# Graph network, three layers on one core: self edges squeezed out of the edge lists of layers 1 and 2, and no more row-by-row loads beside the indirect gathers

## The reference, cut to what matters

```python
h = x @ enc_W + enc_b                                    # 12500 x 64
for l in range(3):
    cat = concatenate([h[src], h[dst], edge_features])   # 64 + 64 + 16 columns
    m = relu(cat @ msg_W1[l] + msg_b1[l]) @ msg_W2[l] + msg_b2[l]
    agg = segment_sum(m, dst)
    h = gru_cell(agg, h, ...)                            # sigmoid, sigmoid, tanh
x = layernorm(x + relu(h @ ro_W1 + ro_b1) @ ro_W2 + ro_b2)
```

## Time and profile before

| | us |
|---|---|
| time, median of 3 (lowest, highest) | 6154.56 (6151.95, 6156.73) |
| profiled execution, first to last instruction | 9775.6 |
| PE busy | 2880.1 |
| DVE busy | 3532.6 |
| ACT busy | 346.4 |
| POOL busy | 4639.2 |

### The profile page before, as it was taken

The page is one execution under the profiler, slowest core; times in us unless marked ns, Lnnn a source line. Parts: engine busy times, 40 slices in busy tenths (PEclk is TensorE's granted clock), DMA queues, the critical chain, the costliest instruction groups (busy, mean ns, idle before and its releaser), DMA issues.

```text
span 9775.6 us, 72182 instructions
## 1 busy us (share of the span) xinstructions
PE 2880.1 (29%) x7290; PEld 1610.2 (16%) x7290; DVE 3532.6 (36%) x4656; ACT 346.4 (4%) x542; POOL 4639.2 (47%) x4865
## 2 busy tenths in 40 slices
PE   3323322322322332222222222223232222322223
PEld 2111111111111221111111111112111111111112
DVE  2333333333333433333333333333333334333334
ACT  0000000000000000000000000000000000000001
POOL 5444444444444454444444444445454445545543
PEclk6555555555555555555555555555555555555555
DMA  3111111111111111111111111111111111111111
GB/s 87 31 31 30 30 30 30 28 31 30 31 30 30 30 28 30 30 30 30 30 30 29 30 30 27 30 31 30 30 31 31 30 30 34 31 31 31 31 30 25
DMA packets 351443, 308.63 MB, mean 32 GB/s; under 512 B 149364, under 2 KB 237518, under 8 KB 350568
## 3 DMA queue, kind: packets, MB, share of 16 engines
q0 software_dynamic: 155328, 159.79, 8.6%
q1 hardware_dynamic: 118271, 110.17, 4.0%
q10 hardware_dynamic: 77328, 33.96, 1.4%
HBM read 280.52 MB, written 22.83 MB: 31 GB/s over the span
## 4 chain that ended last, share of the span: by engine, by line
SPq 57%; issue 38%; DVE 2%; PE 1%; another core or an unknown queue 1%; DMA 0%; ACT 0%; POOL 0%; DVEq 0%; ACTq 0%; POOLq 0%
SPq L473 46%; SPq L469 6%; SPq L642 2%; SPq L633 1%; SPq L527 1%; DVE work_ps L1493 1%; SPq L630 1%; DVE folds L1528 0%; DVE p_src L1490 0%; PE bank L838 0%; DMA p_src<-p_tab 0%; PE work_ps L949 0%; PE bank L962 0%; SPq L662 0%
## 5 line engine op out<-in xcount | busy, mean ns | idle before, releaser
L798 POOL DMA_INDIRECT p_src<-p_tab,idx_all x4767 | 4551.1, 955 | 4916.8 <-DVE work_ps L1493 3467.4
L962 PE MATMUL bank<-hot,folds 128*128 128x96 f32 x2496 | 660.1, 413 | 4012.9 <-issue 2053.0
L1490 DVE TENSOR_TENSOR p_src<-work_ps,p_src 128x512 f32<-128x512 f32 x624 | 427.6, 685 | 3374.9 <-DMA p_src<-p_tab 2912.1
L962 PEld LDWEIGHTS bank<-hot,folds 128*128 128x128 f32 x2496 | 532.1, 296 | 4278.5 <-issue 2198.0
L949 PE MATMUL work_ps<-w_edges,msg 128*128 128x512 f32 x1248 | 1120.0, 997 | 21.4 <-DMA windows_sb<-q_tab 21.4
L1523 DVE SCALAR_TENSOR_TENSOR work_ps<-work_ps,rel 128x1024 f32<-128x1024 f32 x624 | 768.8, 1232 | 21.5
L1493 DVE TENSOR_TENSOR work_ps<-p_src,bank 128x1024 f32<-128x1024 f32 x624 | 767.0, 1229 | 21.4
L1528 DVE TENSOR_REDUCE folds<-work_ps 128x256 f32<-128x1024 f32 x624 | 758.4, 1215 | 0.0
L959 PE MATMUL bank<-hot,counts 128*34 128x96 bf16 x416 | 68.9, 261 | 2248.6 <-issue 1278.6
L1538 DVE TENSOR_TENSOR sums<-bank,sums 128x96 f32 x624 | 158.1, 253 | 872.6 <-remote 699.5
L959 PEld LDWEIGHTS bank<-hot,counts 128*34 128x34 bf16 x416 | 27.1, 108 | 2368.2 <-issue 1359.8
(11 more groups left out here) (167 smaller groups left out, 1800.9 us busy)
## 6 DMA issues: line engine op xcount, KB each, us to landing
p_src<-p_tab ACTq DMA_DIRECT2D x9792, 0.2 KB
p_src<-p_tab SPq DMA_DIRECT2D x9792, 0.2 KB
p_src<-p_tab,idx_all POOLq DMA_INDIRECT x4830
msg<-in_edge_k SPq DMA_DIRECT2D x156, 256.0 KB
pick<-rel_tab SPq DMA_DIRECT2D x312, 96.0 KB
windows_sb<-q_tab ACTq DMA_DIRECT2D x312, 24.0 KB
windows_sb<-q_tab SPq DMA_DIRECT2D x312, 24.0 KB
pick<-q_tab ACTq DMA_DIRECT2D x312, 24.0 KB
```

The costliest lines, as they stand in the source:

```text
L798: pool.indirect_dma_start(out=p_src[r][0:rows, t, :], out_offset=None, in_=p_tab[l][0:NODES, :], in_offset=bass.IndirectOffsetOnAxis(ap=id ...
L962: last = nc.tensor.matmul(fold_ps, folds[:, b, :], hot_all[n % 2][:, s * BLOCKS + b, 1:WINDOW + 1], start=(b == 0), stop=(b == BLOCKS - 1))
L1490: nc.vector.tensor_tensor(rows, edge_ps[k % 2], rows, ALU.add).then_inc(with_edge, 1)
```

## The change

**Packs.** In layers 1 and 2 the edges are cut into 197 packs of 1080 consecutive edges. The self edge of each node is squeezed out of a pack, and what is left (at most 1024 edges) is one step. So layers 1 and 2 have 197 steps, layer 0 still 208 (`STEPS_OF`).

**Squeezing.** It is done on the DVE in layer 0, beside its steps. The edge list is laid out with a pack a partition: 100 packs in a first batch, 97 in a second. For each batch 18 planes of 1080 elements (relative destination, source, 16 features) are moved left by 7 predicated copies each, by 1, 2, 4 ... 64 elements; masks `moves` say which elements take part. `press_step(m)` gives every step of layer 0 its share: 16 steps of a batch make the masks (`prepare`), and then 4 steps a plane: two copies, two, three, and one that turns the plane (`press_plane`). That is 22 groups a batch, 44 of 52 groups in all. SP stores the planes to HBM (`pack_store`), loads the next (`pack_load`), and brings indices and destinations back into SBUF in 8 pieces (`piece_load`), from which `make_masks` makes the masks.

**Self edges.** Their message needs no gather, as source and destination are one node: `h` times (source part + destination part) of the weights, plus the features. Their features are picked out in layer 0 (`select_loops`, a group at a time; two more matmuls and one more DVE add a step) and kept in free rows of `state`. In layers 1 and 2 a chunk has one stage more, -1: a matmul with `loop_w` and a relu on ACT; the DVE adds it to the sums (`loop_added`).

**Single rows.** `single_rows` is gone from SP and ACT; every tile is gathered by GpSimd. Layer 0 has 1661 gathers, layers 1 and 2 have 1576 each.

**Start.** Before the flags are set which choose the branch, the DVE measures whether the packs are within bounds (two loads of 106 rows of the edge list, some 50 more instructions), and the PE's matmuls for the ranges come after the encoder's last unit instead of at its 20th.

```diff
+PACK = 1080
+PACKS = -(-EDGES // PACK)
+BATCHES = ((0, 100), (100, PACKS - 100))
+STEPS_OF = (STEPS, PACKS, PACKS)
...
-        def gathers_of(m):
-            return LAST_TILES if m == STEPS - 1 else EDGE_TILES - has_singles(m)
+        def gathers_of(l, m):
+            return LAST_TILES if l == 0 and m == STEPS - 1 else EDGE_TILES
...
-                    for g in range(2, GROUPS):
-                        single_rows(sp, mybir.EngineType.SP, l, GROUP * (g - 2) + GROUP - 1, 0, SP_ROWS, sp_singles)
-                        group_inputs(n0 + g, g)
+                    for g in range(2, GROUPS_OF[l]):
+                        if l == 0:
+                            batch, at = job(g - 3)
+                            if batch is not None and at >= PREP_GROUPS:
+                                pack_store(batch, at)
+                            batch, at = job(g - 1)
+                            if batch is not None and (at > PREP_GROUPS or (batch, at) == (1, 0)):
+                                pack_load(batch, at)
+                        for q in range(PIECES_ALL):
+                            if piece_loaded_at(q) == (l, g):
+                                piece_load(q)
...
+                        group_inputs(l, n0 + g, g)
                         group_windows(l, n0 + g, g)
...
-                        for at, q in pieces_at(m):
-                            single_rows(act, mybir.EngineType.Activation, l, at, SP_ROWS + q * PIECE, PIECE, act_singles)
...
-                if u == RANGES_AFTER:
-                    pe.wait_ge(vw_sb, LAYERS)
...
+            pe.wait_ge(vw_sb, LAYERS)
+            pe.wait_ge(reduced, 1)
...
+            measured_by(nc.vector.tensor_tensor(rise, pair_dst[:, RUN:], whole, ALU.subtract))
+            measured_by(nc.vector.tensor_reduce(pair_flags[0:PAIRED + 1, 0:1], rise, AX.X, ALU.max))
...
+            def select_loops(n):
...
+                nc.vector.tensor_tensor(edge_major[n % 2], edge_major[n % 2],
+                                        loop_runs[:].unsqueeze(2).to_broadcast([128, GROUP * BLOCKS, EDGE_DIM, RUN]), ALU.mult).then_inc(loop_steps, 1)
+                nc.vector.tensor_reduce(loop_sel[n % 2], edge_major[n % 2], AX.X, ALU.add).then_inc(looped, 1)
...
+            def shift(what, k, count):
+                low, high, by = PASS_LOW[k], PASS_HIGH[k], 1 << k
+                squeeze(nc.vector.copy_predicated(what[0:count, low:high], moves[k][0:count], what[0:count, low + by:high + by]))
...
+            def press_plane(batch, at, part):
...
+                if part < 2:
+                    shift(what, 2 * part, count)
+                    shift(what, 2 * part + 1, count)
+                elif part == 2:
+                    for k in range(4, SHIFTS):
+                        shift(what, k, count)
+                else:
+                    dve.wait_ge(packed, 16 * n)
...
+                        squeeze(nc.vector.tensor_copy(home[0:count].rearrange("p (b g r) -> p b g r", b=BLOCKS, g=RUN),
+                                                      what[0:count, 0:STEP].rearrange("p (b r g) -> p b g r", b=BLOCKS, g=RUN)))
...
+                if j == 0 and l:
+                    dve.wait_ge(loop_act, nth_loop(l, c) + 1)
+                    dve.wait_ge(kept, last_of(l, c) + 1)
+                    nc.vector.tensor_tensor(chunk_sum[0:HID, 0:w], zr[0:HID, 0:w], sums[0:HID, at + 1:at + 1 + w], ALU.add).then_inc(loop_added, 1)
...
+                        if l == 0:
+                            press_step(m)
```

More of the change, by code:

```diff
@@ L78 @@
 ENC_PAIRS = PAIRS + 1
-RANGES_AFTER = 20
 UNITS = 2 * ENC_PAIRS
@@ L476, in pieces_at, with where @@
-        def pieces_at(m):
-            due = [(m + AHEAD_OF - q, q) for q in range(PIECES)]
-            if m == 0:
-                due = [(GROUP - 1, q) for q in range(PIECES) if GROUP - 1 + q <= AHEAD_OF]
-            return [(at, q) for at, q in due if at < STEPS and has_singles(at)]
-        def nth_single(l, m):
-            return l * SINGLES + m // GROUP
-        def chunk_stages(m):
+        def where(k):
+            l = sum(k >= first for first in FIRST_STEP[1:])
+            return l, k - FIRST_STEP[l]
@@ new lines, in group_of, with begun, job, pressed_by @@
+        def group_of(l, m):
+            return FIRST_GROUP[l] + m // GROUP
+        def begun(n):
+            l = sum(n >= first for first in FIRST_GROUP[1:])
+            return FIRST_STEP[l] + min(GROUP * (n - FIRST_GROUP[l]), STEPS_OF[l])
+        def job(group):
+            batch, at = divmod(group - FIRST_JOB, BATCH_GROUPS)
+            return (batch, at) if 0 <= batch < len(BATCHES) else (None, None)
+        def pressed_by(group):
+            batch, at = job(group)
+            if group < FIRST_JOB:
+                return 0
+            if batch is None:
+                return sum(PREP_OPS) + len(BATCHES) * (BATCH_GROUPS - PREP_GROUPS) * PLANE_OPS
+            before_it = sum(PREP_OPS[0:batch]) + batch * (BATCH_GROUPS - PREP_GROUPS) * PLANE_OPS
+            return before_it + PREP_OPS[batch] + (at + 1 - PREP_GROUPS) * PLANE_OPS
@@ new lines, in _ @@
+            measured_by(last)
+            for i, (_, bound) in enumerate(MOST + LEAST):
+                last = nc.vector.tensor_scalar(measured[:, :, i], measured[:, :, i], float(bound), None, ALU.is_gt if i < len(MOST) else ALU.is_lt)
+            measured_by(last)
+            measured_by(nc.vector.tensor_reduce(pair_flags[0:PAIRED, 4:5], measured.rearrange("p j i -> p (j i)"), AX.X, ALU.add))
+            measured_by(nc.vector.tensor_scalar(far[:], row_f[:], 2.0 * PACK_RATE, -PACK_SLACK, ALU.mult, ALU.add))
@@ new lines, in press_step, with make_masks @@
+            def press_step(m):
+                batch, at = job(m // GROUP)
+                if batch is None:
+                    return
+                if at < PREP_GROUPS:
+                    prepare(batch, at * GROUP + m % GROUP)
+                else:
+                    press_plane(batch, at, m % GROUP)
+            def make_masks(q):
+                first, end = packs_of(q)
+                count = (end - first) * BLOCKS
+                runs = pieces_i[q % 2][:, 0:end - first].rearrange("p u (b g) -> p (u b) g", g=RUN)
+                here = slice(first * BLOCKS, end * BLOCKS)
+                lead_edge = runs[:, :, 0:1].to_broadcast([128, count, RUN])
+                dve.wait_ge(piece_in[q % 2], 16 * BLOCKS * (q // 2 + 1))
+                nc.vector.tensor_copy(rel_first[:].rearrange("p u b -> p (u b)")[:, here], runs[:, :, 0])
+                nc.vector.tensor_tensor(masks[:, here, 0, :], runs, lead_edge, ALU.is_equal)
+                nc.vector.scalar_tensor_tensor(masks[:, here, 1, :], runs, -1.0, lead_edge, ALU.add, ALU.is_equal).then_inc(remasked, 1)
+                dve.wait_ge(remasked, q + 1)
@@ L1473, in landed @@
             def landed(k):
[L1475 removed]
+                return 16 * sum(gathers_of(*where(j)) for j in range(k % ROW_SLOTS, k + 1, ROW_SLOTS) if j >= PRE)
             def edge_sums(k):
```

551 lines of the change are left out of this document (427 added, 124 removed).

## The result

The changed kernel took 6276.1 us (median of 4, 6273.6 to 6279.6) against 6155.3 for the kernel before: ratio 1.0197, 95% interval [1.0183, 1.0212]. The forecast was 6233, with bounds of 6185 and 6285. Its direction and its mechanism held; the cost of the mechanism was 1.6 times the forecast.

What follows compares the result with a forecast made beforehand. GpSimd's gathers were taken to bound all three layers; on the median of 6154.6 us, -21 (fewer gathers) + 86 (stretched gathers) + 5 (layers 1 and 2) + 8 (start) gave 6233 us, bounds 6185 to 6285.

Steps and rivals of the forecast that it cites:

- What bounds: All layers: GpSimd's gathers, 1.257 us from start to start, bound the kernel before; 39 us a group where SP needs 30.
- SP and ACT bound the kernel before: Rival: the profile's chain holds in plain execution too, so the change is much faster, 5944 us; chance 8%.
- Number of gathers: All layers: 4813 gathers for 4830, 17 fewer at 1.257 us, -21 us.
- DVE's work hidden: Layer 0: the DVE needs 37.3 us a group against 40.2 for gathers, so its new work itself costs nothing.
- What it does to the gathers: Layer 0: DVE instructions with two SBUF inputs block gathers that start beneath them; +86 us, bounds 0 and 130.
- Turns: Layer 0: the copy that turns each plane has one input and costs the gathers 0.10 us, between 0 and 0.12.
- Predicated copies: Layer 0: each pair costs the gathers 0.61 us, three narrowing ones 0.48; with the turn 1.8 a plane, 65 for 36.
- DMAs: SP's plane transfers and the 8 pieces: 0, covered by slack; without that cover up to 20 us each, 160 in all.
- Start: Before layer 0: the DVE's measures and later range matmuls delay the start by 0 to 18 us, taken as +8.
- No blocking: Rival, layer 0: predicated copies don't hold gathers; 6134 to 6160 us if nothing or little blocks; chance 21%.
- two clocks an element: Rival, layer 0: predicated copies take two clocks an element, 295 us instead of 86, about 6440 in all; chance 6%.
- stalls at pieces: Rival: pieces or layer changes stall GpSimd after all, +20 to +80 us, 6250 to 6310; chance 11%.

Runs made afterwards that it cites:

- A run with more records: Changed kernel with single rows put back in all three layers and turns on ACT (73,914 instructions on record): 6457.9 us against 6155.1 for the kernel before.
- The one-input multiplication: Changed kernel with every predicated copy replaced by an in-place multiplication by 1.0: 7380.7 us against 9782.1 for the kernel before, on a second-kind chip.

## Why the prediction was right, and where it was off

*What bounds.* Right: GpSimd in all layers, and the single rows hidden. Wrong was the reason given for the span of 9775.6 us. I held that recording stops the queues. A run with more records has none of it, and executions without a profile take as long on two chips. The sum from undisturbed stretches held since GpSimd's rhythm is the same on both kinds. The kernel before has no trace from the first kind, so that GpSimd bounds it there rests on that sum and on the 1.2 us a gather that single rows saved in layers 1 and 2. The rival "SP and ACT bound the kernel before" wasn't false either: it is true for chips of the second kind. There the changed kernel itself was not run; with its turns on ACT it takes 7372 to 7387 for 9782 to 9803.

*Number of gathers.* -21 stands in the balance above.

*DVE's work hidden.* Right: GpSimd never waits for it in layer 0, on the first kind of chip.

*What it does to the gathers.* The mis-sized step: 86 forecast, 138 measured, above even the upper bound of 130. By its terms:
- Turns: 0.10 each was forecast, 3.6 us; they cost 21.5, 0.6 each. I had taken for a small effect of one-input instructions. The row shows 0.12 lost to a 0.59 us instruction in 16-bit form; it was no measure of a f32 copy of 1.07 us, which also holds a gather that started up to 0.5 us before it.
- Predicated copies: 61 for the planes and a part of the masks' 15, 104 measured. There are two parts. First, they hold a gather until about 0.16 us before their end, some 1.23 us of 1.39, for 1.15 forecast. The row of L1604 in the earlier trace rows had it already: the gather beside it went on 0.59 us into an instruction of 0.76, while the element part, by which I went from the two rows of L1577, would be 0.44. With the measured durations and chance meetings a plane's seven copies come to about 2 us (forecast 1.70), an estimate of 71 to 75 us for 36; the gathers that started under a copy lost 71, masks included. So chance was a fair picture for these. Second, I had put the loss of a gather already under way at nothing, without a reason. 20 of them lost 31 us, 1.5 each.
- Masks and `select_loops`: 15 and 6 forecast, 10 (beside their predicated copies) and 1 measured. The tensor_tensor of `select_loops` had 5 gathers start under it, and 51 that were under way when it began lost 0.02 us together.

The sum came out nearer than its terms: the gathers cost 52 us more than forecast, layers 1 and 2 and the start together 13 less, with 4 us left over. That makes the 43 us by which the forecast was short. That the smaller errors went against the large one was luck.

The Trainium skill ("SBUF — State Buffer", "SBUF: two separate sides") has the holder keep the interface for the whole instruction. With 0.15 to 0.17 us of the end excepted, the gathers that start under a copy agree, and better than with my element part: by its rule the prediction put layer 0 at 110. The same sentence gives the interface to whichever starts first. The 20 gathers under way that predicated copies held, and the 30 that turns held, had started first by their records, so for them the trace doesn't agree, or a gather's record begins before it needs the interface.

The Trainium skill (the same page, "Who interferes with whom") says that copies with one input can hold both ports in their fast mode. The one-input multiplication, 0.73 us for 1092 elements, and its held gathers agree; the prediction had the rule and gave it 4 us. The turn held gathers in the same way (they ended 0.12 us after either), but its 1.07 us for 1024 elements doesn't show whether it ran in that mode.

*Layers 1 and 2.* +5 forecast; the windows show 0 (1487 us for 1560 gathers in each).

*DMAs.* 0 was right, with the cover named. The bound of 160 was for pieces that come late without that cover; what came late without it were the 16 planes of the second batch, at 250 us beside single rows. That such a plane keeps SP's queue for 22.5 us in the changed kernel too, the prediction didn't foresee; it stayed hidden.

*Start.* +8 forecast, about 0 measured: what is left in the balance for start, tail and layers 1 and 2 together is 4 us. The stall of 13.6 in the earlier trace rows that should have hidden part of it comes from a trace of the second kind of chip; whether the kernel before has it on the first, no run shows.

*The rivals.* No blocking is refuted by the run without copies, two clocks an element by copies of 1.30 and 1.41 us, and stalls at pieces by GpSimd's rows, which have no other wait over 1 us.

## What to carry to other kernels

Before moving work to an idle engine, ask what it touches: here the DVE had room for 9.2 us of work a plane (2.85 + 2.82 + 2.49 + 1.07), and the squeezing still took 136 us of the engine that bounds, through SBUF. In these runs an operand in PSUM (no gather of layer 0 was stretched beside such an instruction alone) and another engine (the turns on ACT, layer 0 shorter by 33.7 us) took it off. To start a little after the bound engine's instruction is no safe way: 77 of 97 such gathers were left alone by predicated copies, but 4 of 34 by the turns. When a profile's span and the plain time differ by half, look for another explanation than the recorder: find an instruction that can't be slow, such as a register move, and see its maximum.

## What the runs showed of the hardware, unexpected

- Chips differ: register moves on SP and ACT of 29 ns with a maximum of 42 ns on some, 1444 ns on others; a kernel with 19,584 single-row loads takes 6155 or 9782 to 9803 us.
- A strided f32 copy of 1024 elements (1.07 us) on the DVE holds a gather that began 0.03 to 0.51 us before it until 0.12 us after its own end (30 gathers), and leaves one alone that began 0.57 us or more before (4 gathers).
- A predicated copy mostly doesn't (77 gathers, 0.95 us), but it held 20 that had begun 0.08 to 0.67 us before it, for 1.5 us each; these ended 0.79 to 0.81 us after the copy. Which gathers it holds stays open.
- A reduction of 512 f32 elements from SBUF to SBUF (0.69 us) holds none: 26 gathers started under it and lost 0.06 us together.
- Issuing a load of 100 rows of 4320 bytes keeps SP's queue for 0.67 us at the median, one of 97 rows for 22.5 (changed kernel, 16 loads each).
- A predicated copy takes 1.30 us for 1094 bytes and 1.41 for 1094 f32 values a partition.
